# Gated cross-attention block: the last six quarters of the attention ask for their column scores in pairs

## What is computed

```python
def _L0_xattn_ref(q, k, v):
    scores = jnp.einsum('bkgsd,bktd->bkgst', qh, kh) / scale
    weights = jax.nn.softmax(scores, axis=-1)
    out = jnp.einsum('bkgst,bktd->bkgsd', weights, vh)
...
x = x + jnp.tanh(g_xattn[0]) * _L0_xattn_ref(_layernorm(x, axis=-1), ctx_512, ctx_512)
x = x + jnp.tanh(g_ffn[0]) * _L0_ffn_ref(_layernorm(x, axis=-1), L0_ffn_w_gate, L0_ffn_w_up, L0_ffn_w_down)
```

## Time and profile before

| | us |
|---|---|
| median of 3 runs | 476.5 |
| lowest and highest run | 476.45, 476.8 |
| profiled execution, from its first to its last instruction (span) | 474.1 |
| TensorE busy, with matrix products | 459.7 |
| VectorE busy | 390.8 |
| ScalarE busy | 293.0 |
| GpSimd busy | 211.3 |

### The profile page before, as it was taken

The page is one execution under the profiler, slowest core; times in us unless marked ns, Lnnn a source line. Parts: engine busy times, 40 slices in busy tenths (PEclk is TensorE's granted clock), DMA queues, the critical chain, the costliest instruction groups (busy, mean ns, idle before and its releaser), DMA issues.

```text
span 474.1 us, 8995 instructions
## 1 busy us (share of the span) xinstructions
PE 459.7 (97%) x3110; PEld 299.1 (63%) x3130; DVE 390.8 (82%) x745; ACT 293.0 (62%) x465; POOL 211.3 (45%) x314
## 2 busy tenths in 40 slices
PE   7999999999999999989999999999999999999997
PEld 7665656566566434458954469864468874479664
DVE  4889988788978739968998977999894999889892
ACT  4478886667868677787547507653616653647470
POOL 4245455978887544555005834202925300930000
PEclk9999999999999999999999999999999999999999
DMA  7999110121012014000100551100362110153086
GB/s 228 322 348 345 42 50 12 24 57 25 13 40 94 18 29 167 1 0 14 24 11 1 100 146 33 22 11 0 66 123 76 24 24 0 22 92 66 0 137 219
DMA packets 68183, 35.90 MB, mean 76 GB/s; under 512 B 50288, under 2 KB 62960, under 8 KB 68144
## 3 DMA queue, kind: packets, MB, share of 16 engines
q1 hardware_dynamic: 67728, 34.61, 28.2%
q10 hardware_dynamic: 416, 0.79, 0.5%
HBM read 19.26 MB, written 4.19 MB: 49 GB/s over the span
## 4 chain that ended last, share of the span: by engine, by line
PE 73%; DVE 13%; issue 7%; ACT 3%; POOL 2%; DMA 1%; DVEq 0%; POOLq 0%; ACTq 0%
PE ps L817 14%; PE ps L611 10%; PE ps L594 9%; PE ps L871 9%; PE ps L637 7%; PE ps L894 6%; PE ps L654 4%; PE ps L883 2%; PE ps L885 2%; PE ps L761 2%; DVE wst L1401 2%; PE ps L619 2%; PE ps L691 2%; DVE y_split L1376 2%; DVE st L1196 1%
## 5 line engine op out<-in xcount | busy, mean ns | idle before, releaser
L817 PE MATMUL ps<-wst 128*128 128x512 bf16 x499 | 111.7, 379 | 3.3 <-DVE wst L1396 2.1
L1233 DVE TENSOR_REDUCE reg<-ps 128x4 f32<-128x512 f32 x128 | 81.9, 684 | 24.4 <-PE ps L611 23.3
L817 PEld LDWEIGHTS ps<-wst 128*128 128x128 bf16 x512 | 49.1, 98 | 62.1 <-DVE wst L1396 4.2
L611 PE MATMUL ps<-reg 32*128 32x256 f32 x512 | 86.7, 400 | 0.6 <-DVE reg L1233 0.2
L968 ACT ACTIVATE reg<-ps 128x1024 f32<-128x1024 f32 x64 | 65.4, 1022 | 35.0 <-PE ps L619 34.8
L556 POOL TENSOR_TENSOR reg_rest<-reg_rest,z_sc 128x1024 f32<-128x1024 f32 x24 | 47.3, 2009 | 84.7 <-DVE z_sc L1438 84.7
L1100 ACT ACTIVATE wst<-wst 128x512 f32<-128x512 f32 x64 | 40.0, 626 | 51.8 <-DVE wst L1396 51.5
L594 PE MATMUL ps<-reg 32*128 32x512 f32 x256 | 71.9, 639 | 0.0
L871 PE MATMUL ps<-had_f,wst 128*128 128x128 f32 x512 | 67.1, 276 | 1.1 <-DVE wst L1401 1.1
L871 PEld LDWEIGHTS ps<-had_f,wst 128*128 128x128 f32 x512 | 64.0, 191 | 4.3 <-DVE wst L1401 1.8
L611 PEld LDWEIGHTS ps<-reg 32*128 32x128 f32 x512 | 58.7, 184 | 5.5 <-issue 1.0
(11 more groups left out here) (164 smaller groups left out, 745.3 us busy)
## 6 DMA issues: line engine op xcount, KB each, us to landing
wst<-in_w SPq DMA_DIRECT2D x16, 512.0 KB, 8.1
reg<-in_w SPq DMA_DIRECT2D x8, 512.0 KB, 4.9
out<-x_all SPq DMA_DIRECT2D x16, 256.0 KB, 2.1
x_all<-in_x SPq DMA_DIRECT2D x3, 1024.0 KB, 9.1
reg<-in_k_t SPq DMA_DIRECT2D x32, 32.0 KB, 2.3
reg<-in_v SPq DMA_DIRECT2D x4, 256.0 KB, 4.0
x_all<-in_x ACTq DMA_DIRECT2D x1, 512.0 KB, 4.4
reg_rest<-reg SPq DMA_TRANSPOSE x20, 3.1
```

Of the source, the lines that this page charges most:

```text
L611: last = pe.matmul(ps[:, row_banks(r) + m, 256 * g:256 * g + 256], q_t[n % 4][strip(i), P * h:P * h + P], kpad[n // CHUNK % 2][strip(i), n ...
L817: last = pe.matmul(ps[:, banks[ob % n], :], tern_gu[:, ob // 2, m, j, P * (ob % 2):P * (ob % 2) + P], q1_t[:, j, :], start=(j == 0), stop= ...
L1233: dve.tensor_reduce(neg_max[n % 2][:, g:g + 2, i + m, :], ps[:, row_banks(r) + m, :].rearrange("p (g a t) -> p g a t", g=2, a=2), AX_X, AL ...
```

## The change

Up to quarter 57 nothing changes. The last six quarters, c = 58 to 63 (`LONE = QUARTERS * NB - 6`), are asked for in three pairs by a new function `column_pair(b, j)`: fp32 products of quarter c on strips 0 and 1, those of quarter c + 1 on strips 2 and 3, then the selector products of both in the same order. Each half has its own wait for the exponential that frees its banks, and its own cols_done. The pairs go round three pairs of banks: 2 and 3, 0 and 1, 4 and 5 (0 and 1 held row scores until quarter 56). `last_steps` writes out TensorE's order for batches 14 and 15.

```diff
@@ -199,6 +199,14 @@
+        LONE = QUARTERS * NB - 6
+
+        def column_bank(c):
+
+            if c < LONE:
+                return C_BANKS + 2 * (c % 2)
+            return (2, 0, 4)[(c - LONE) % 3]
+
...
-                a, bank = j // 2, C_BANKS + 2 * (j % 2)
+                a, bank = j // 2, column_bank(c)
...
+            def column_pair(b, j):
+
+                c, a = QUARTERS * b + j, j // 2
+                if c == LONE:
+                    pe.wait_ge(sem("max_done"), 2 * QUARTERS * NB)
+                for k in range(2):
+                    pe.wait_ge(sem("exp_done"), c + k - (1 if c + k == LONE else 2))
+                    for m, i in enumerate((2 * k, 2 * k + 1)):
+                        pe.matmul(ps[:, column_bank(c + k) + m, :], kpad[b // CHUNK % 2][strip(i), b % CHUNK, a, :],
+                                  q_t[b % 4][strip(i), :], start=True, stop=False)
+                m_ready(pe, b)
+                for k in range(2):
+                    for m, i in enumerate((2 * k, 2 * k + 1)):
+                        last = pe.matmul(ps[:, column_bank(c + k) + m, :], sel[strip(i), a, :], m_t[b % 2][strip(i), :],
+                                         start=False, stop=True)
+                    last.then_inc(sem("cols_done"), 1)
...
+            def last_steps():
+
+                b = NB - 2
+                quarter(b, 0)
+                weigh(b - 1, 1)
+                early_had(b)
+                quarter(b, 1)
+                turn_out(b - 1, 0)
+                column_pair(b, 2)
+                weigh(b, 0)
+                turn_out(b - 1, 1)
+                b = NB - 1
+                column_pair(b, 0)
+                weigh(b - 1, 1)
+                turn_out(b - 1, 0)
+                column_pair(b, 2)
+                weigh(b, 0)
+                early_second(b)
+                turn_out(b - 1, 1)
...
-            for b in range(NB):
+            for b in range(NB - 2):
                 step(b)
+            last_steps()
...
-                bank = C_BANKS + 2 * (j % 2)
+                bank = column_bank(c)
```

## The result

The changed kernel took 474.38 us (median of 20 runs, 474.06 to 474.75), the kernel before 476.51 (20 runs beside them). The ratio is 0.9951, with a 95% interval of 0.9941 to 0.9961: faster by 2.1 us. One of the 20 runs before took 482.97 us, the other 19 between 476.00 and 477.03; with it or without it the median is 476.5. The forecast was 474.5, with faster as the likely case.

The account below looks back on a forecast made before the run. TensorE was taken to bound the stretch; 3.84 us removed, less about 0.3, 0.3 and 1.2 of waits, left 2.0 (1.97 by the turn's start), so 476.5 - 1.97 = 474.5 us, range 473.9 to 476.0.

Parts of the forecast that it names:

- Four strips at once: TensorE, last six quarters: a pair takes 1.28 us where two quarters took 2.56; three pairs take off 3.84 us.
- The rival of partial overlap: Four strips only partly overlap, or selector products follow each other: 0.2 to 0.3 us once, 474.7 to 474.8; chance 0.14.
- both 0.66 us waits: ScalarE's idle times before the exponentials of quarters 59 and 61, waiting for selector products; both were to go.
- TensorE's new wait: TensorE idle from 172.85 to 174.06, some 1.2 us, before `turn_out(14, 1)`, until ScalarE's copy L1058 has read the bank.
- the turn: TensorE's start of `turn_out(14, 1)`, taken to set the phase's end: from 176.03 to 174.06, 1.97 us earlier.
- its ledger: TensorE's sum: 3.84 us removed, less about 0.3 in the third pair, 0.3 before weighing (15, 0), 1.2 before the turn: 2.0.
- ScalarE's gap from a copy to the next exponential: In ScalarE's queue: exponentials placed at 166.80 and 170.27, the first 0.58 us behind the copy at 166.22.
- The floor of 2.1 us: Most ScalarE's queue can lose: 2 x 0.66 us plus 0.8 from copy to turn, giving 474.4 us.
- The waits held for met: Pairs find row maxima and turned maxima ready, the nearest 0.8 us ahead; the late-pairs rival, 475 to 476.5, chance 0.06.
- the third pair's second half: TensorE: needs quarter 60's exponential, ending 169.78, so starts at 169.93, while the first half starts at 169.54.
- The rival of a gain given back: Behind the attention, later stages keep their old time and half or all is lost: 475.5 to 476.5; chance 0.12.
- The slower rival: Four strips do not overlap: a pair takes 2.56 us, the turn comes 0.55 later, 477.05 us or more; chance 0.06.

Follow-up runs that it names:

- same_strips: Changed kernel with both halves of each pair on strips 0 and 1, same number and sizes of products: 476.68 us, ratio 1.000 to the kernel before.
- first_pair: Changed kernel with only quarters 58 and 59 as a pair, batch 15 in its old order of single quarters: 475.54 us, ratio 0.9974 to the kernel before.
- last_pair: Changed kernel with only quarters 62 and 63 as a pair, on banks 0 to 3, all before in old order: 475.95 us, ratio 0.9983 to the kernel before.
- two_pairs: Changed kernel with the third pair taken apart, quarter (15, 3) placed after the ones-times-diagonal product: 474.51 us, ratio 0.9955 to the kernel before.
- late_loads: Changed kernel with the last four weight loads held until the last exponential is done: 474.08 us, ratio 0.995 to the kernel before.
- halves_apart: Changed kernel with each pair's first-quarter scores and selectors written before the second quarter's, on their own strips: 474.42 us, ratio 0.9956 to the kernel before.

## Why the prediction was right

**Four strips at once.** Right in each part: 1.28 us for a pair as read from the earlier trace rows, nothing extra for the selectors. same_strips shows that this overlap is the cause, by taking it alone away. The rival of partial overlap falls: the scores take 0.96 us to the selectors' start for four products, and 0.97 for two. The Trainium skill (TensorE: Matmul & The Clock Gate, Measured speedup vs the span model) has four tiles of 32 rows at 3.07 times the speed of one; the prediction's estimate from it, 1.30 times as long, does not fit these rows. The earlier trace rows held less than I read from it: the 256-column products there start one after the other, at 146.00, 146.16, 146.31 and 146.48, so that it showed the price of that many columns, and not four strips starting at once.

**Who sets the pace next.** Right: both 0.66 us waits went, ScalarE's queue is full, and its copy ends TensorE's new wait, foreseen at 1.2 us and measured at 1.20. Both its ends came some 0.2 us sooner than foreseen, since both hang on quarter 61's exponential; the wait between them kept its length. first_pair and last_pair came out at the turns that the same working gave: 1.26 us earlier for one, 0.64 for the other. What the prediction did not say, though its ledger held it, is that the third pair's saving and the new wait are the same time: two_pairs does as well without it.

**The size of the shift.** 1.97 us foreseen, 2.19 measured. The term that was mis-sized is ScalarE's gap from a copy to the next exponential. I took the copy's whole 0.58 us, from rows where idle time followed it. Where the exponential lies ready, it starts 0.49 us behind the copy's start (166.62 to 167.11) and 0.46 at 169.97. Two of those are 0.21 us, nearly the whole difference of 0.22. The floor of 2.1 us, which the prediction took as the most that could be gained, has the same fault: the turn moved by 2.19.

**From span to time.** I carried 2.4 us from the span to the median. The changed kernel's runs lie 1.8 us above their spans (472.5 and 474.27 in one of them). So the profiled execution of before was some 0.6 us shorter than a middling one. The spans differ by 1.6 us, the medians by 2.13, the turns by 2.19. Of the 0.6 us between spans and turns, 0.39 lie ahead of quarter 57 and the rest behind the stage, within the scatter given above. The forecast held since the shift was subtracted from the median and not taken from the spans.

**The waits held for met** were met: the maxima, the turned maxima, the third pair's second half. I had that half start 0.39 us behind the first; it started 0.20 behind (170.14 against 169.94). One reason is the delay of 0.15 us that I took for TensorE behind whatever releases it. It holds for the turn (the copy ends at 174.08, the turn starts at 174.23), but the second half started 0.06 us behind the end of quarter 60's exponential (170.08), and the weighing 0.05 behind that of quarter 61's (171.49 to 171.54). All of this fell into the wait for the copy, as foreseen. Two smaller slips changed nothing: the first pair needs quarter 56's exponential, not quarter 57's, and the first gate block takes 1.82 us from its start to the weighing (174.69 to 176.51), not 1.60, since the row of the kernel before shows seven of its eight products.

**The gain stayed**, all of it, to the stage behind the gates, and by the medians to the end. The rival of a gain given back falls with that, and late_loads leaves the earlier loads no share. The granted clock stayed at 1.00 across the 1.20 us stand.

**The slower rival** was priced too high: the world without overlap is a tie at 476.68, not 477.05. Its point of decision, a pair of 2.3 us, was right; its length of 2.56 us was not, since two halves in a row take 2.35.

## What to carry to other kernels

When a step is made shorter, work out the queue that paces it next and every copy whose cover was the work that went; here one line moved on two engines was worth 1.4 us more, and without it the last third of the change was worth nothing. Look for the price of a new overlap in a stretch where the kernel already does it. Take gaps between instructions from a place where the queue is full, not from a length that idle time follows.

## What the runs showed of the hardware that was not expected

Score products on strips 2 and 3 started 0.01 to 0.03 us behind those on strips 0 and 1, though two bf16 products that had to wait were written between them (halves_apart, first pair: eight records in 1.15 us, the selectors 0.97 us behind the first). A pair's two halves on the same strips took 2.35 us, against 1.28 on four strips and 2 x 1.28 for two quarters that stand apart. Behind the end of a ScalarE instruction that released it, TensorE started a turn after 0.15 us, and products after 0.05 to 0.06.
